# A transformer block on one core: two-part fp16 attention operands, and three PSUM banks in turn for S, S^T and the small stages

## The reference, cut to what matters

```python
x = x + 0.5 * ffn(layernorm(x), gate_w, w_gate, w_up, w_down)
x = x + attn(layernorm(x), rms_w, Wq, Wk, Wv, Wo)
x = x + 0.5 * ffn(layernorm(x), gate_w, w_gate, w_up, w_down)

def attn(x, ...):
    xn = rms_norm(x, rms_w)
    q, k, v = heads(xn @ Wq), heads(xn @ Wk), heads(xn @ Wv)
    scores = where(causal, einsum('bshd,bthd->bhst', q, k) / 16, -inf)
    probs = softmax(scores)
    return einsum('bhst,bthd->bshd', probs, v) @ Wo + x

def ffn(x, ...):                      # each token goes to the expert with the larger logit
    sel, top_w = argmax(softmax(x @ gate_w.T)), max(softmax(x @ gate_w.T))
    h = silu(x @ w_gate[sel].T) * (x @ w_up[sel].T)
    return (h @ w_down[sel].T) * top_w
```

## Time and profile before

| | |
|---|---|
| median of 3 runs | 1332.26 us (1330.32 to 1336.48) |
| the profiled execution | 1319.46 us |
| its span, first to last instruction | 1317.7 us |
| mean granted clock of TensorE | 0.95 |
| PE busy | 1096.0 us, 83% |
| DVE busy | 960.4 us, 73% |
| ACT busy | 711.8 us, 54% |
| POOL busy | 527.7 us, 40% |

### The profile page before, as it was taken

The page is one execution under the profiler, slowest core; times in us unless marked ns, Lnnn a source line. Parts: engine busy times, 40 slices in busy tenths (PEclk is TensorE's granted clock), DMA queues, the critical chain, the costliest instruction groups (busy, mean ns, idle before and its releaser), DMA issues. The chain is left out here.

```text
span 1317.7 us, 39560 instructions
## 1 busy us (share of the span) xinstructions
PE 1096.0 (83%) x14564; PEld 946.3 (72%) x14564; DVE 960.4 (73%) x2040; ACT 711.8 (54%) x1331; POOL 527.7 (40%) x663
## 2 busy tenths in 40 slices
PE   0787789968999888888788898997979989788895
PEld 0766667757778776777676687876867878677784
DVE  6545547796888878878878887888878888675431
ACT  4434315655566565655655665675646655555321
POOL 3154443254523344443334533334543253343432
PEclk9898889998999899999899899998999999889998
DMA  9120352213221124123222141112422112311111
GB/s 319 58 81 26 105 93 60 86 54 86 74 83 48 34 70 114 39 66 91 69 75 74 54 126 51 39 57 67 100 74 61 52 51 72 82 47 42 50 45 45
DMA packets 115665, 96.16 MB, mean 73 GB/s; under 512 B 52288, under 2 KB 109376, under 8 KB 115488
## 3 DMA queue, kind: packets, MB, share of 16 engines
q1 hardware_dynamic: 98400, 66.88, 18.3%
q0 software_dynamic: 6144, 16.79, 4.3%
q10 hardware_dynamic: 10944, 9.97, 2.4%
HBM read 45.75 MB, written 37.88 MB: 63 GB/s over the span
## 5 line engine op out<-in xcount | busy, mean ns | idle before, releaser
L620 POOL TENSOR_TENSOR h_lo<-hid,h_hi 128x256 bf16<-128x256 f32 x304 | 221.2, 748 | 515.3 <-ACT h_hi L684 514.9
L760 ACT ACTIVATE area<-ps_st 128x512 f32<-128x512 f32 x320 | 190.5, 595 | 288.2 <-PE ps_st L1166 285.2
L953 DVE TENSOR_REDUCE row_min<-ps_s 128x1 f32<-128x512 f32 (+2 forms) x384 | 183.5, 505 | 79.2 <-PE ps_s L1145 78.0
L1077 PE MATMUL ps_g<-x_t,w 128*128 128x128 f16 x1104 | 211.5, 226 | 16.0 <-issue 8.8
L1079 PE MATMUL ps_u<-x_t,w 128*128 128x128 f16 x1104 | 211.5, 225 | 0.0
L1079 PE MATMUL ps_g<-x_t,w 128*128 128x128 f16 x1104 | 211.3, 226 | 0.0
L1077 PE MATMUL ps_u<-x_t,w 128*128 128x128 f16 x1104 | 211.1, 225 | 0.0
L1078 PE MATMUL ps_g<-x_t,w 128*128 128x128 f16 x1104 | 210.6, 225 | 0.0
L1078 PE MATMUL ps_u<-x_t,w 128*128 128x128 f16 x1104 | 209.9, 223 | 0.0
L971 DVE TENSOR_TENSOR area<-area 128x512 f16<-128x512 f32 x256 | 199.3, 779 | 9.7 <-ACT area L761 9.6
L1143 PE MATMUL ps_s<-kt,qt 96*128 96x512 bf16 (+3 forms) x512 | 139.6, 311 | 73.1 <-DVE row_min L953 56.8
(11 more groups left out here) (162 smaller groups left out, 2847.1 us busy)
## 6 DMA issues: line engine op xcount, KB each, us to landing
qk_scratch<-area SPq DMA_DIRECT2D x32, 384.0 KB, 2.6
qt<-qk_scratch SPq DMA_DIRECT2D x192, 64.0 KB, 2.7
kt<-qk_scratch SPq DMA_DIRECT2D x192, 64.0 KB, 2.7
y_sorted<-ys ACTq DMA_DIRECT2D x76, 128.0 KB, 1.7
x_buf<-x SPq DMA_DIRECT2D x8, 512.0 KB, 4.8
out<-x_buf SPq DMA_DIRECT2D x8, 512.0 KB, 2.9
x_sorted<-yt SPq DMA_DIRECT2D x18, 128.0 KB, 1.9
area<-w_down SPq DMA_DIRECT2D x4, 512.0 KB, 13.7
```

Source lines behind the costliest of these rows:

```text
L620: pool.tensor_tensor(h_lo[:, u % 2, c], hid[:, u % 2, c], h_hi[:, u % 2, c], ALU.subtract).then_inc(h_lo_done, 1)
L760: act.activation(p_f32[:, f % 3], ps_st[:], ACT.Exp, scale=-1.0)
L953: ins = dve.tensor_reduce(row_min[:, p % 2, h + hh, i:i + 1], ps_s[:, at:at + P * (i + 1)], AX.X, ALU.min)
L1077: pe.matmul(cols, w_hi, x_hi, start=kb == 0 and f == 0, stop=False, skip_group_check=True)
```

## The change

**Parts.** q, k and v are written as two fp16 parts instead of three bf16 ones. The `proj_rest` stage goes (L741, L745, L935, L941); ACT writes part 1 and DVE part 2 straight from PSUM. Four products of parts fill 64 rows instead of 96; S is taken over 65 rows and ST over 68. PV's moving operand has 33 columns instead of 49. The stores of q and k carry 256 KB instead of 384, and a part is loaded by 8 DMAs instead of 12. So that fp16 holds the values, the attention weights are scaled by a power of two: a third `w_scale` at point 23, with two reduces of 768 columns, and a scale from a tile in the exps (`s_scale`) instead of the constant -1.0.

**Banks.** `ps_s`, `ps_st` and `ps_m` become `ps_w[0..2]`. Every stage of S, ST and the small ones takes the next one in PE's order, and waits for what was done with the stage three places back. The `SPARE` units use the two `ps_v` banks instead, and one more unit is among them (the last of pass 1); the first late one waits for the last `o_norm`, the first PV for the early ones.

**Reduces.** The fills with pieces of 384 and 128 columns are laid out as four blocks of 128 and reduced by one instruction with four results; a small reduce once a part combines them.

**x_update.** It stands 16 points after the end of a pass instead of 13, but ahead of the norm that needs it; `yt` gets a second buffer, so that a gather waits for the update before the last.

**Ones.** The memset that writes the ones beside k's parts is made after unit 8 instead of 19, now also one for q's row of zeros; the first loads of q and k wait for it.

Tanh, hid, row_min and exp get stages of their own in the plan, at the points they had.

```diff
-QPART = [0, 1, 2, 0, 1, 0]
-KPART = [0, 0, 0, 1, 1, 2]
+QPART = [0, 1, 0, 1]
+KPART = [0, 0, 1, 1]
 ROWS = HD * len(QPART)
-VW = 3 * HD + 1
+MAX_ROWS = 3
+MAX_AT_ROW = ROWS + 1
+VW = 2 * HD + 1
...
-ONES_UNIT = 19
-SPARE = [u for u, (n, s, q) in enumerate(UNITS)
-         if q == 1 and n in (0, 1, len(PASSES) - 1) and (n, s) != (1, SLOTS[1] - 1)]
+ONES_UNIT = 8
+SPARE = [u for u, (n, s, q) in enumerate(UNITS) if q == 1 and n in (0, 1, len(PASSES) - 1)]
...
-S_FILLS = [[(0, 3, 0)], [(1, 3, 0)], [(0, 2, 0), (0, 0, 384)], [(1, 2, 0), (1, 0, 384)], [(0, 1, 0), (1, 1, 256)]]
+S_FILLS = [[(0, 3, 0)], [(1, 3, 0)], [(0, 0, 0), (0, 2, 128)], [(1, 0, 0), (1, 2, 128)], [(0, 1, 0), (1, 1, 256)]]
...
-SCALE_AT = [-50.5, 3.9]
+SCALE_AT = [-50.5, 3.9, 23]
...
-        put(end + 8, "y_gather", k)
-        put(end + 13, "x_update", k)
+        put(end + GATHER_LAG, "y_gather", k)
+        at = end + UPDATE_LAG
+        if what == "first":
+            at = min(at, part_at(GROUPS * b, NORM_AT[0]) - 1)
+        put(at, "x_update", k)
...
-        free, last = {}, None
+        bank_of, free, turns = {}, {}, [None, None, None]
         for st in order:
-            if st[0] in ("transpose", "proj", "out_proj", "row_max", "l_prefix", "w_scale"):
-                free[st] = last
-                last = {"transpose": lambda b, kind, kb: (xt_lo_done, 2 * sets[b, kind] + kb + 1),
-                        "proj": lambda b, m: (rest_done, NP * b + m + 1),
...
+            if st[0] in ("transpose", "proj", "out_proj", "row_max", "l_prefix", "w_scale", "scores", "scores_t"):
+                n = len(free)
+                bank_of[st], free[st] = ps_w[n % 3], turns[n % 3]
+                turns[n % 3] = {"transpose": lambda b, kind, kb: (xt_lo_done, 2 * sets[b, kind] + kb + 1),
+                                "proj": lambda b, m: (part2_done, NP * b + m + 1),
...
+                                "scores": lambda p, f: (max_done, FILLS * p + f + 1),
+                                "scores_t": lambda p, f: (exp_done, FILLS * p + f + 1)}[st[0]](*st[1:])
...
-                    if n:
-                        pool.wait_ge(x_updated, n)
+                    if n >= 2:
+                        pool.wait_ge(x_updated, n - 1)
...
-                    pool.memset(kt[ROWS:ROWS + 3].bitcast(F32), TWO_ONES).then_inc(ones_ready, 1)
+                    pool.memset(qt[ROWS:ROWS + 1].bitcast(F32), 0.0)
+                    pool.memset(kt[ROWS:ROWS + 1 + MAX_ROWS].bitcast(F32), TWO_SCALES).then_inc(ones_ready, 1)
...
-                    act.activation(p_f32[:, f % 3], ps_st[:], ACT.Exp, scale=-1.0)
-                    act.activation(p_hi[:, f % 4], ps_st[:], ACT.Exp, scale=-1.0).then_inc(exp_done, 1)
+                    act.activation(p_f32[:, f % 3], ps[:], ACT.Exp, scale=s_scale[:])
+                    act.activation(p_hi[:, f % 4], ps[:], ACT.Exp, scale=s_scale[:]).then_inc(exp_done, 1)
...
+                    elif k == 2:
+                        dve.scalar_tensor_tensor(out=rms_abs[:], in0=rms_col[:], scalar=-1.0, in1=rms_col[:],
+                                                 op0=ALU.mult, op1=ALU.max)
+                        for kb in range(KB):
+                            w = GU_PIECES + DOWN_PIECES + kb
+                            dve.wait_ge(w_in[w], 16)
+                            ins = dve.tensor_reduce(wa_max[:, kb:kb + 1], stage[w][:, 0:WO], AX.X, ALU.max,
+                                                    apply_absolute_value=True)
+                        link(ins)
...
-                        for hh, i, at in S_FILLS[f % KINDS]:
-                            ins = dve.tensor_reduce(row_min[:, p % 2, h + hh, i:i + 1], ps_s[:, at:at + P * (i + 1)],
-                                                    AX.X, ALU.min)
+                        ins = dve.tensor_reduce(minima[:, kind - 2, :, 0], ps[:].rearrange("p (j n) -> p j n", j=T),
+                                                AX.X, ALU.min)
...
-                    if FILLS * p + f:
-                        pe.wait_ge(max_done, FILLS * p + f)
-                    else:
-                        pe.wait_ge(gated, LAST_EARLY + 1)
...
-                    if FILLS * p + f:
-                        pe.wait_ge(exp_done, FILLS * p + f)
```

More of the change, by code:

```diff
@@ L244, in macaron @@
         ys = [sb(f"ys{n}", [P, D], F32) for n in range(2)]
-        yt = sb("yt", [P, T, D], F32)
+        yt = [sb(f"yt{n}", [P, T, D], F32) for n in range(2)]
         xt_hi = sb("xt_hi", [P, KB, S], F32R)
@@ L319, in macaron @@
         w_two16 = sb("w_two16", [1, 2], BF16)
-        w_scale = sb("w_scale", [P, 2, 2], F32)
+        w_scale = sb("w_scale", [P, 3, 2], F32)
         g_scale = sb("g_scale", [P, 1], F32)
         y_scale = sb("y_scale", [P, 1], F32)
+        s_scale = sb("s_scale", [P, 1], F32)
         ps_g, ps_u, ps_y = bank("ps_g"), bank("ps_u"), bank("ps_y")
-        ps_s, ps_st, ps_m = bank("ps_s"), bank("ps_st"), bank("ps_m")
+        ps_w = [bank(f"ps_w{n}") for n in range(3)]
         ps_v = [bank(f"ps_v{n}") for n in range(2)]
         ps_o = [v[:, 0:2 * T * VW].rearrange("p (h i c) -> p h i c", h=2, i=T) for v in ps_v]
-        qk_scratch = nc.dram_tensor("qk_scratch", [2 * HALVES, 3, HH, HD, S], BF16, kind="Internal").ap()
-        max_scratch = nc.dram_tensor("max_scratch", [GROUPS, 3 * HG * T, P], BF16, kind="Internal").ap()
+        qk_scratch = nc.dram_tensor("qk_scratch", [2 * HALVES, 2, HH, HD, S], F16, kind="Internal").ap()
+        max_scratch = nc.dram_tensor("max_scratch", [GROUPS, MAX_ROWS * HG * T, P], F16, kind="Internal").ap()
         x_sorted = [nc.dram_tensor(f"x_sorted{n}", [PLACES, 2 * D], F16, kind="Internal").ap() for n in range(2)]
@@ L642, in _ @@
                     act.wait_ge(w_in[w], 16)
-                    scale = 1.0
-                    if w < GU_PIECES + DOWN_PIECES:
-                        of = w // GU_PIECES
-                        act.wait_ge(w_scale_done, of + 1)
-                        scale = w_scale[:, of, 0:1]
-                    act.activation(split[w][0], stage[w], ACT.Copy, scale=scale).then_inc(w_hi_done, 1)
+                    of = 2 if w >= GU_PIECES + DOWN_PIECES else w // GU_PIECES
+                    act.wait_ge(w_scale_done, of + 1)
+                    if of < 2:
+                        ins = act.activation(split[w][0], stage[w], ACT.Copy, scale=w_scale[:, of, 0:1])
+                    else:
+                        for inv, cols in enumerate((slice(0, WO), slice(WO, WO + D))):
+                            ins = act.activation(split[w][0][:, cols], stage[w][:, cols], ACT.Copy,
+                                                 scale=w_scale[:, of, inv:inv + 1])
+                    ins.then_inc(w_hi_done, 1)
                 elif what == "l_norm":
@@ L669, in _ @@
                     act.activation(e_abs[:], neg_abs[:], ACT.Exp, scale=1.0 / XSCALE).then_inc(l_exp, 1)
-                elif what == "gate" and st[2] == KB - 1:
+                elif what == "tanh":
                     u = st[1]
@@ L715, in _ @@
                     scale = rms_col[:, kb:kb + 1] if kind == "attn" else 1.0
-                    act.activation(xt_hi[:, kb, :], ps_m[:], ACT.Copy, scale=scale).then_inc(xt_hi_done, 1)
+                    act.activation(xt_hi[:, kb, :], ps[:], ACT.Copy, scale=scale).then_inc(xt_hi_done, 1)
                 elif what == "proj":
@@ L792, in _ @@
                     dve.wait_ge(w_two_out, k + 1)
-                    ins = dve.tensor_copy(w_scale[:, k], ps_m[:, 0:2])
+                    ins = dve.tensor_copy(w_scale[:, k], ps[:, 0:2])
                     if k == 0:
@@ L812, in _ @@
                     else:
-                        ins = dve.tensor_tensor(split[w][1], stage[w], split[w][0].bitcast(F32), ALU.subtract)
+                        for inv, cols in enumerate((slice(0, WO), slice(WO, WO + D))):
+                            ins = dve.scalar_tensor_tensor(out=split[w][1][:, cols], in0=stage[w][:, cols],
+                                                           scalar=w_scale[:, 2, inv:inv + 1],
+                                                           in1=split[w][0][:, cols].bitcast(F32), op0=ALU.mult,
+                                                           op1=ALU.subtract)
                     ins.then_inc(w_ready, 1)
@@ L874, in _ @@
                     ins.then_inc(x_updated, 1)
-                elif what == "up" and st[2] == KB - 1:
+                elif what == "hid":
                     u = st[1]
@@ L1045, in _ @@
                     for m in range(T):
-                        ins = pe.matmul(ps_m[:, m + 1:T + 1], ones[:], sel0[i][:, 0:T - m], start=False,
+                        ins = pe.matmul(ps[:, m + 1:T + 1], ones[:], sel0[i][:, 0:T - m], start=False,
                                         stop=m == T - 1, skip_group_check=True)
@@ L1128, in _ @@
                         at = (WQ if kind == "q" else WK) + g * P
```

(2 more changed lines are left out.)

255 lines of the change are left out of this document (132 added, 123 removed).

## The result

| | before | changed kernel |
|---|---|---|
| median | 1333.54 us (1330.32 to 1336.48) | 1291.51 us (1289.34 to 1293.70) |
| profiled execution | 1319.46 us | 1289.34 us |
| its span | 1317.7 us | 1287.6 us |
| PE busy | 1096.0 us | 1091.3 us |
| DVE busy | 960.4 us | 905.7 us |

The ratio of the medians is 0.9685, 95% interval 0.9655 to 0.9716: 42 us faster. The prediction was 1262 us in a range of 1226 to 1308. So the sign and the range held, and the size was 28 us off: a gain of 70 us was forecast from the median then known (1332.26), and 42 came.

The account below looks back on a forecast made before the run. PE, in-order, was held mostly by S waiting for its one bank behind DVE's row_min. Terms -45 -20 -13 -2 +6 -6 +12, and -2 for unit 19, gave -70: 1249.5 profiled, 1262 us median, range 1226 to 1308.

Parts of the forecast that it names:

- The slower rival (S on ACT): S fills would wait for late exps on ACT, each of 320 fills paying; 1350 us; chance 0.08.
- the waits move: DVE's in-order queue paces the middle; PE, freed at S, waits at ps_g, down and PV; 1302 us; chance 0.17.
- turn of the banks, with small stages, exp slack, clock: PE's bank waits: S -45, small stages -20; ST's exp wait -4; fewer PE cycles at 1.2 GHz -6 us.
- what comes back: Stages behind DVE's bursts (gate banks, down, PV) wait more once PE no longer stands at S: +12 us, 0 to 40 possible.
- x_update and second yt: DVE idles less for gathered rows, so long S waits behind it shrink: -13 us, between 5 and 20 gained.
- third w_scale: At the start, PE waits for a DVE chain in pass 0: +6 us, bounds +2 and +9.
- longer exps: On ACT, a scale from a tile lengthens each exp from 595 to about 680 ns: +2 us.
- two fp16 parts, reduces; also unit 19's pair of banks, the memset of the ones: DVE about 50 us lighter but no term; unit 19's banks -2 us; memset on POOL nothing, up to +4.
- Three banks in turn: S, ST and small stages wait for the stage three places back; S waits in PE fall by 45 us.
- So the 38 short waits (29 us) go: S waits of PE for row_min, some 0.8 us each, vanish because S has 1.6 us more for its reduce.
- PV: Narrower moving operand, 49 to 33 columns, on PE: 0 us taken, bounds 0 to 17.
- the clock: With some 80 us fewer pauses PE cools less often: 6 us back, bounds 0 and 15.

Follow-up runs that it names:

- the step of -10: From the kernel before with only the banks in turn (1294.53 us) to the changed kernel with x_update back at 13 points and one yt (1284.48 us).

## Why the prediction was right, and where it was off

**The sign** held, and so did most of what was to show it. S waits for row_min fell from 72.9 to 10.5 us, DVE's wait at `x_update` by two thirds, the exps take 686 ns, PV's cadence is unchanged, DVE is 55 us lighter. But one sign failed: PE's waits for `row_min` were to fall "from 73 to under 20 us", and they are 36.0 in all, since ST has 22.6 of them (34.2 and 36.4 us in the profiles on the first and the second chip). **The mechanism** held in part: the banks in turn were to carry nearly all of the gain and carry some half of it. The slower rival (S on ACT) did not come: S waits for an exp 0.5 us in all. Nor did "the waits move" as drawn, at DVE as the pace of the middle; they moved on a smaller scale, to ST, and PE's wait for `h_lo` grew from 8.2 to 11.6 us (15.3 and 15.8 on the first and the second chip). The price of that rival has a slip: a third of the gain of 70 would be 23 us and 1309, not 30 and 1302.

**The sum** was -70. It is best tested on the first and the second chip, whose kernel before (1319.3 and 1317.7) is that of the profile on which the sum was made (1319.5): there the changed kernel takes 1260.3 us, -59 and -57. So the sum is 11 to 13 us off, in terms that err more than that in both directions: that it came so near is luck. The steps on the first chip, 1319.3, 1294.5, 1284.5, 1260.4:

| term | forecast | measured |
|---|---|---|
| turn of the banks, with small stages, exp slack, clock | -45 -20 -4 -6 | -25 on the kernel before, -29 on the changed one |
| what comes back | +12 | contained in these |
| x_update and second yt | -13 | -24 |
| third w_scale | +6 | +6 |
| longer exps | +2 | +3, within the noise |
| two fp16 parts, reduces; also unit 19's pair of banks, the memset of the ones | no term; -2, 0 | -19: the rest of the step of -10, after +6 and +3 |

1. *Three banks in turn* failed in size: with what comes back the forecast was -63, and -25 to -29 came. The step that broke is "where only S and ST alternate it now has one and a half, 4.7 us: 1.6 us more", and with it "So the 38 short waits (29 us) go". I asked only what S gains by a third bank, and never what ST pays: the one price I put at nothing was PE's wait for the exp of ST. In the turn the ST two places on takes the bank of an S and waits for its row_min. Nor does it come half a fill later. The plan puts ST at 31 + 1.05 points behind the S of its own fill, and 31 is no whole number of fills of 2.1 points, so each ST stands 0.55 points (0.8 us) behind some S and not 1.05. (In the profile with only the turn, an ST starts 1.1 us after the S before it and an S 1.7 us after the ST before it, both in the median.) A reduce thus has one fill and 0.8 us until PE wants its bank, not one fill and 1.6 us. The run with only the turn shows it: eleven long waits (over 1.9 us) of 43.9 us in all are ten of 37.2, where 28 us (43.9 - 16) should have been left, and the 38 short ones of 29.0 us are 31 of 20.3, where none should have been. All in all 15 us went and not 45, and 41.8 of the 57.5 us left are at ST. The long wait followed above lost 0.9 us (4.62 to 3.76) even with a lighter DVE.
2. *x_update* was mis-sized in the other direction, 24 against a bound of 20, and the reason given ("It lies on PE's path only through DVE's queue") was incomplete. On the kernel before the later place gives 5 us, on the changed one the place some 17 and the second buffer 7. So the edits are not additive. My reading is that an idle DVE costs little while S has one bank and waits anyway, and costs more once it does not. That is argued, not shown: no run has the later place with the turn alone, so the lighter DVE may be the reason as well, and the 17 is a difference between two chips.
3. *The parts* were not costed at all ("That is no term of its own, since DVE is not the bound"), and are worth up to some 19 us, together with the small edits in the same step. This is worked out from several measured times, each uncertain by some 5 us, on two chips, so its size is rough; but the step itself is 10 us faster although it holds the third `w_scale` and the longer exps. Between the two profiles of the step PE's waits for row_min fell from 57.5 to 45.2 us. An engine that is not the bound on average still is in its bursts.
4. *The start* (+6; the first S is 6.1 us earlier without it, and yet the first S of the changed kernel stands only 1 us later than before, because the turn of the banks alone had brought it forward by 5), *the exp* (+2 and 3), and *PV* (0) came as worked out. For *the clock* I took 6 us back: PE's busy time fell by 4.7 us in the first profile of the changed kernel (granted clock 0.95 and 0.951), by 19.7 and 10.7 us on the first and the second chip (1076.3 and 1085.3 us), and not at all on the third (1096.0). Single profiled executions differ by more than the term, so it is neither shown nor excluded.
5. *From the profiled execution to the median.* I added 12.8 us as an offset that both kernels have. The experiments show what it most likely is: the kernel before takes 1318 to 1319 us on two chips and 1337 on the third, and the median before (1332.3) lay near the third, the profile near the others. On that kind of chip the changed kernel loses 30 us (1260 to 1290), more than the kernel before with some 19. That the first measurement ran on such a chip is an inference from its issue waits (33.4 us, as on the third) and its time; its chip is not known. This difference of 11 us and the 12 us of the sum make up 23 of the 28 us. The last 5 are the difference between the gain on the third chip (47 us, ratio 0.9593 to 0.9691) and in the first measurement (42 us, 0.9655 to 0.9716), whose intervals overlap.

**What stays open:** what stops PE beside POOL's indirect DMAs on the third chip, and why that chip costs the changed kernel 11 us more than the one before. The issue waits themselves are as large in both (34.3 us in the kernel before with the later x_update). They are also not all: from the second to the third chip the span of the changed kernel grew by 27.1 us, 10.7 of them in PE's busy time.

## What to carry to other kernels

When stages of several kinds take banks in one turn, write down for each kind whose bank it takes, and at what distance in the plan: its wait becomes one for another stage's reader, and a burst on that reader is paid by whoever is next in line. Then look for what makes the burst long before making more room for it; here moving one GpSimd operation out from under four small VectorE operations was worth as much as the turn of the banks (31 us on the third chip against 25 to 29 on the first). Price an edit on the state of the kernel that the other edits leave: the same move of `x_update` gave 5 us on the kernel before and some 17 on the changed one.

## What the runs showed of the hardware

- PE pauses of 0.25 to 2 us with no releaser, 39 of 41 beside an indirect DMA of POOL, on one of three chips; on the other two the same program had two such pauses, none beside one. A program without any change was 30 us (1260 to 1290) apart between chips. So kernels 2% apart can be compared only on the same chip.
- A VectorE product of 256 columns with two SBUF inputs, 0.42 us alone, takes 2.22 to 2.36 us when it starts 0.1 to 0.5 us into a GpSimd operation of 2.1 to 2.6 us on SBUF, and 1.25 us when it starts 0.36 us into one of 1.33 us (`p_lo`, in the run with dlogit later). In every case it ends 0.28 or 0.29 us after that operation.
- A reduce of 512 fp32 columns from PSUM costs 683 to 688 ns whether it gives one, two or four results; split in 384 and 128 columns it cost 830.
